# Two gather passes of a graph network on 16 of 17 edge tiles for 22 node blocks, each node's edge to itself taken from the products

## The reference, cut to what matters

```python
loop = jnp.arange(3125)
src = jnp.concatenate([s, d, loop]); dst = jnp.concatenate([d, s, loop])
o = jnp.argsort(dst, stable=True); src, dst = src[o], dst[o]

x = ln(x + gin(x))          # 4 times: h = x + segment_sum(x[src], dst); x = relu(h@W1+b1)@W2+b2
x = ln(x + rgcn(x))         # kinds of edge_type_8, each kind's mean, x@root
x = ln(x + attentive(x))    # srcs = alphas[rels] * (x @ w_rel)[rels, src], segment-summed; + x@update per edge
x = ln(x + gated(x))        # msg = (x@W + bias)[rel, src] * sigmoid(gate), segment-summed; + x@loop
```

## Time and profile before

| | |
|---|---|
| median of 3 runs | 2251.13 us (2251.12 to 2251.75) |
| the profiled execution, own time | 2252.56 us |
| its span | 2250.8 us |
| busy share of PE, PEld, DVE, ACT, POOL | 65%, 44%, 40%, 27%, 60% |
| chain that ended last | POOL 50%, PE 21%, issue 18%, ACT 5% |
| L1013 on POOL, passes 2 and 3 | 832 gathers, 954 ns each |
| L1315 on PE, the dense layers | 2100 matmuls, 406.8 us |

### The profile page before, as it was taken

One profiled execution on the slowest core, in us unless ns is written; L12 is line 12 of the kernel. 1 busy time (PEld: TensorE's weight loads), 2 busy tenths in 40 slices (PEclk: granted clock), 3 DMA queues, 4 the chain that ended last, 5 costly groups with the idle time before them and its releaser, 6 DMA issues.

```text
span 2250.8 us, 31616 instructions
## 1 busy us (share of the span) xinstructions
PE 1463.2 (65%) x7538; PEld 989.7 (44%) x7539; DVE 906.3 (40%) x2269; ACT 599.7 (27%) x1689; POOL 1360.4 (60%) x1574
## 2 busy tenths in 40 slices
PE   4776999999987777777764655555455433434433
PEld 2332554545456665666653533343333333323333
DVE  7887122213673444444445533333344212212212
ACT  3776000000023333333331644444343000000000
POOL 5000166720007777777777777777777777777775
PEclk8888999999988989989897876667677756565565
DMA  1000011100213333333333222222222222222221
GB/s 31 0 0 10 15 9 12 11 3 0 59 54 109 94 113 112 95 112 110 95 113 97 72 81 79 71 80 79 71 81 84 56 56 56 55 56 56 55 56 46
DMA packets 126652, 137.49 MB, mean 61 GB/s; under 512 B 80706, under 2 KB 97866, under 8 KB 123433
## 3 DMA queue, kind: packets, MB, share of 16 engines
q0 software_dynamic: 40896, 81.94, 13.9%
q1 hardware_dynamic: 85673, 54.54, 8.1%
HBM read 91.88 MB, written 44.52 MB: 61 GB/s over the span
## 4 chain that ended last, share of the span: by engine, by line
POOL 50%; PE 21%; issue 18%; ACT 5%; DVE 2%; ACTq 1%; DMA 1%; POOLq 1%; SPq 0%; DVEq 0%
POOL adj L1013 49%; PE acc L1315 18%; ACT adj L1714 5%; PE misc L1251 1%; PE acc L1586 1%; PE acc L1202 1%; ACTq L1707 1%; DVE adj L2607 0%; DMA adj<-table,adj 0%; DVE adj L2606 0%; ACTq L1714 0%; POOLq L1009 0%; PE acc L1251 0%; ACT adj L1773 0%; PE acc L1204 0%
## 5 line engine op out<-in xcount | busy, mean ns | idle before, releaser
L1013 POOL DMA_INDIRECT adj<-table,adj x832 | 793.5, 954 | 253.6 <-issue 252.9
L1586 PE MATMUL acc<-adj 128*128 x1760 | 364.5, 385 | 499.7 <-DMA adj<-table,adj 253.3
L1586 PEld LDWEIGHTS acc<-adj 128*128 128x128 f32 x1760 | 328.5, 285 | 560.3 <-issue 560.2
L1013 POOL DMA_INDIRECT adj<-tablex,adj x416 | 392.8, 944 | 210.9 <-issue 126.5
L1773 ACT ACTIVATE adj<-adj 128x128 f32<-128x128 f32 x832 | 264.5, 390 | 581.0 <-DMA adj<-tablex,adj 315.2
L1315 PE MATMUL acc<-adj,feat 128*128 (+1 forms) x2100 | 406.8, 354 | 8.4 <-issue 8.4
L1513 PE MATMUL acc<-adj 128*128 128x128 f32 x1664 | 245.3, 310 | 124.1 <-ACT adj L1773 113.9
L1997 DVE TENSOR_TENSOR adj<-acc,drel 128x768 f32<-128x768 f32 (+1 forms) x148 | 139.9, 948 | 423.6 <-PE acc L1586 423.3
L1513 PEld LDWEIGHTS acc<-adj 128*128 128x128 f32 x1664 | 228.8, 220 | 167.2 <-issue 167.1
L1315 PEld LDWEIGHTS acc<-adj,feat 128*128 (+1 forms) x2100 | 186.2, 98 | 217.1 <-issue 13.1
L959 POOL TENSOR_TENSOR node_rep<-node_rep,compb 128x128 f32<-128x128 f32 x128 | 58.5, 457 | 272.4 <-DMA node_rep<-in_L_gnn_weight_dram 263.5
(11 more groups left out here) (352 smaller groups left out, 1297.6 us busy)
## 6 DMA issues: line engine op xcount, KB each, us to landing
table<-adj SPq DMA_DIRECT2D x24, 1024.0 KB, 4.1
adj<-table,adj POOLq DMA_INDIRECT x834, 2.5
table<-adj SPq DMA_DIRECT2D x25, 512.0 KB, 2.9
adj<-tablex,adj POOLq DMA_INDIRECT x416, 2.5
table<-adj SPq DMA_DIRECT2D x25, 64.0 KB, 2.0
out_dram<-adj SPq DMA_DIRECT2D x24, 64.0 KB, 1.5
temp<-in_x_dram SPq DMA_DIRECT2D x4, 256.0 KB, 3.1
wrel<-node_rep SPq DMA_DIRECT2D x16, 64.0 KB
```

What stands on the lines that cost most here:

```text
L1013: pool.indirect_dma_start(ring[:, p_, 0:D], None, rows_, bass.IndirectOffsetOnAxis(ap=gidx[:, p_:p_ + 1], axis=0)).then_inc(msgs_in[third_ ...
L1586: last = nc.tensor.matmul(acc[:, bass.ds(blk[s], width)], hot[:, c, j, :], ring_flat[:, bass.ds(place[s], width)], start=False, stop=True, ...
```

## The change

In passes 2 and 3, tile 7 of the turns 2 to 23 (22 of 25; `LB = 2`, `LN = 22`) is no longer gathered, weighted or multiplied. Each of the 128 nodes of that turn's block has its loop edge somewhere in the tiles; the loop edges are taken out of the lists, and the edges of tile 7 are put in their places ("holes"). What a loop edge adds is taken from the products, which are on the chip anyway: `table_parts` picks each node's row of its own kind, 16 chained operations of 128 by 128 a block in pass 1 and 8 in pass 2, and `block_sum` of pass 2 adds the picked row by its weight.

To find the holes, the program now does this beside the dense layers:

- SP loads the list of destinations again, moved by one (`next1_i`, 3 DMAs, now in `ends_in`), waits for all nine, and writes the tiles' first nodes to DRAM; DVE puts five operations more on 104 by 512 into the check.
- DVE packs the edges' codes (`code_lists`); POOL then issues six DMAs, among them every eighth element of the list of destinations to DRAM (6640 pieces of 4 bytes) and two loads of 128 by 22 pieces of 4 bytes, before its first slice.
- Three searches follow, each 22 gathers on POOL (`found_rows`) and some counting on DVE: `loop_nodes`, `loop_eighths` and `loop_holes`. `loop_eighths` stands on DVE ahead of `merge(1)`, and `loop_holes` ahead of `merge(2)`.
- 66 scatters on POOL, three for each emptied tile, each after the last of its kind has landed, put codes and nodes in place. SP then loads them with four DMAs, where there was one.
- `EARLY_SLICES` becomes 9, 4, 3, and the 28 scatters of `edges_part` come after all slices. The load of the moved edges into the lists goes from layer 3 to turn 2 of pass 1, with `loops_taken`.

```diff
-EARLY_SLICES = (range(0, 6), range(6, 11), range(11, 16), ())
+EARLY_SLICES = (range(0, 9), range(9, 13), range(13, 16), ())
...
-                    for j in range(SIZES[c]):
+                    for j in range(SIZES[c] - (1 if c == 1 and emptied(ph, u) else 0)):
...
-                with pool.Fori(0, LAYERS // 2) as l:
-                    for q in range(SLICES // LAYERS):
-                        weights_slice(l, q)
-                pool.wait_ge(late_counted, PLACES_SET)
-                with pool.Fori(LAYERS // 2, LAYERS - 1) as l:
-                    for q in range(SLICES // LAYERS):
-                        weights_slice(l, q)
-                        edges_part(q)
...
+                pool.wait_ge(late_counted, LISTS_SET)
+                pool.dma_start(edge_codes[0:P * TILES, :].rearrange("(p t) o -> p (t o)", p=P)[:, FROM_TILE:TILES], tile16[:, FROM_TILE:TILES]
+                               ).then_inc(loops_in, 16)
+                pool.dma_start(edge_nodes[0:P * STEPS, :].rearrange("(p s) o -> p (s o)", p=P), step_nodes).then_inc(loops_in, 16)
+                pool.dma_start(eighths[0:TILES - 1, :].rearrange("t e -> (t e)"), bass.AP(dst.tensor, dst.offset, [[P // 16, (TILES - 1) * (P // 8)], [1, 1]])
+                               ).then_inc(loops_in, 16)
+                for k, o in ((0, here_i), (1, behind_i)):
+                    pool.dma_start(o, bass.AP(dst.tensor, dst.offset + emptied_tile(0) * P + k, [[1, P], [TPT * P, LN], [1, 1]])).then_inc(edges_in, 16)
+                pool.wait_ge(ends_in, ENDS_IN + 16)
+                pool.wait_ge(loops_in, 3 * 16)
+                pool.dma_start(firsts_b, first_list.partition_broadcast(P)).then_inc(edges_in, 16)
+                slices(0, 9)
+                pool.wait_ge(late_counted, NODES_SET)
+                found_rows(lambda b: sixteen[:, b, :], eighths, row_i)
+                slices(9, 13)
+                pool.wait_ge(late_counted, EIGHTS_SET)
+                found_rows(lambda b: eight[:, b, :], dst[0:E // 8 * 8].rearrange("(r e) -> r e", e=8), row_i)
+                slices(13, 16)
+                pool.wait_ge(late_counted, HOLES_SET)
+                found_rows(lambda b: found[:, b:b + 1], edge_codes, row_i)
+                for n in range(SWAPPED // 4):
+                    edges_part(n)
+                pool.wait_ge(loops_in, 3 * 16 + 3 * LN * 16)
+                for b in range(LN):
+                    if b > 0:
+                        pool.wait_ge(edges_in, (3 + b) * 16)
...
+                    pool.wait_ge(edges_out, (SWAPPED + b) * 16)
...
                 for l in range(LAYERS):
+                    if l == 0 and not general:
+                        code_lists()
                     if l == 1 and not general:
+                        loop_nodes()
                         edge_places()
+                        loop_eighths()
+                    if l == 2 and not general:
+                        loop_holes()
                     if l < LAYERS - 1:
                         merge(l)
...
+                        for r in range(R2):
+                            rows_ = stage[:, b.r, r * D:(r + 1) * D]
...
+                                ins = nc.vector.scalar_tensor_tensor(mine, rows_, of_r, mine, ALU.mult, ALU.add)
```

More of the change, by code:

```diff
@@ L409, in gnn @@
         zerob = sb("zerob", [P, KB], BF16)
+        hole = zerob[:, :].bitcast(F32)
+        here_i, behind_i, slot_c, slot_d, row_i, node_i, found = (hole[:, i * LN:(i + 1) * LN].bitcast(I32) for i in range(7))
+        here_f, node_f, tile_f, place_n, ends_f = (hole[:, i * LN:(i + 1) * LN] for i in (0, 7, 8, 9, 10))
+        more_f, many_f = (place_f[:, i * LN:(i + 1) * LN] for i in range(2))
+        loop_i = late[:, 2 * SWAPPED:2 * SWAPPED + LN].bitcast(I32)
+        assert 11 * LN <= KB // 2 and LN <= SWAPPED and 2 * LN <= 4 * 15
         epst = sb("epst", [P, 1])
@@ L655, in tiles_from, with emptied, picks, full_turns @@
             return u.num(TPT, PARTS_AT[c])
-        def msgs_before(ph, u, c):
-            uses = sum(uses_in(q, third_of(ph, u), c) for q in range(1, ph))
-            return u.third(16 * SIZES[c], 16 * SIZES[c] * uses)
+        def emptied(ph, u):
+            return ph > 1 and (not isinstance(u.k, int) or LB <= u.num() < LB + LN)
+        def picks(b):
+            return not isinstance(b.k, int) or LB - 1 <= b.num() < LB + LN
+        def full_turns(r):
+            return sum(1 for i in (*range(LB), *range(LB + LN, TURNS)) if i % AHEAD_T == r)
+        def tiles_in_pass(ph, r, c):
+            n = uses_in(ph, r, c)
+            if ph == 1 or c != 1:
+                return n * SIZES[c]
+            return n * (SIZES[c] - 1) + full_turns((r - ph + 1) % AHEAD_T)
+        def msgs_upto(ph, u, c):
+            before = sum(tiles_in_pass(q, third_of(ph, u), c) for q in range(1, ph))
+            if ph == 1 or c != 1:
+                return u.third(16 * SIZES[c], 16 * (before + SIZES[c]))
+            full = full_turns(u.r) - (1 if u.r == (TURNS - 1) % AHEAD_T and not u.last() else 0)
+            return u.third(16 * (SIZES[c] - 1), 16 * (before + SIZES[c] - 1 + full))
         def uses_in(ph, r, c):
@@ L1769, in take @@
                     return
-                hold(act, msgs_in[third_of(ph, u)][c], msgs_before(ph, u, c) + 16 * SIZES[c])
-                for j in range(SIZES[c]):
+                hold(act, msgs_in[third_of(ph, u)][c], msgs_upto(ph, u, c))
+                for j in range(SIZES[c] - (1 if c == 1 and emptied(ph, u) else 0)):
                     o = ring[:, place_of(ph, u, c) + j, 0:D]
@@ L2274, in edge_places, with code_lists @@
                 nc.vector.engine_nop().then_inc(late_counted, 1)
+            def code_lists():
+                codes, kind = tile16[:, FROM_TILE:TILES], split[:, 0:TILES - FROM_TILE].bitcast(I32)
+                place(nc.vector.tensor_copy(kind, tile8[:, FROM_TILE:TILES]))
+                place(nc.vector.tensor_single_scalar(kind, kind, R1 - 1, ALU.bitwise_and))
+                nc.vector.tensor_copy(step_nodes, drel[:, :])
+                place(nc.vector.scalar_tensor_tensor(codes, codes, float(R1), kind, ALU.mult, ALU.add))
+                nc.vector.engine_nop().then_inc(late_counted, 1)
@@ L2477, in table_parts @@
                     last.then_inc(rows_set, 1)
+                    if not general:
+                        hold(dve, rows_set, b.num(1, 1))
+                        hold(dve, prod_free[SIDE], blocks_seen(2, b, 1))
+                        for r in range(R3):
+                            if r > 0:
+                                dve.wait_ge(picked, b.num(R3, PICKS2 + r + min(max(b.num(1, 1 - LB), 0), LN)) if isinstance(b.k, int)
+                                            else b.num(R3 + 1, PICKS2 + r + 1 - LB))
+                            nc.vector.scalar_tensor_tensor(own, stage[:, b.r, r * D:(r + 1) * D],
+                                                           own_kind3[:, bass.ds(b.num(), 1), r:r + 1].rearrange("p b r -> p (b r)"), own,
+                                                           ALU.mult, ALU.add).then_inc(picked, 1)
             def one_pass(ph, general):
```

237 lines of the change are left out of this document (198 added, 39 removed).

## The result

The changed kernel took 2485.4 us in the median of 4 runs (2480.8 to 2486.0); the kernel before took 2251.4 beside it (2251.1 to 2253.3). The ratio is 1.103, with a 95% interval of 1.101 to 1.105. The forecast was slower, 2333, between 2305 and 2405: the direction held, the size did not. 234 us were added, not 80.

A forecast was written before the change was run, and what follows sets the result against it. POOL's gathers were taken to bound the passes, PE the stretch before. To 2252.6 us it added 5.0 (start), 93.1 + 25 (POOL's queue and X), 3 (clock), 9.6 (DVE tails), less 55.4 (gathers): 2333, range 2305 to 2405.

The forecast's parts named there:

- Where it is decided: On POOL before pass 1: clearing `near_i` stands behind the new work, comes 93.3 us + X late, and delays pass 1.
- three signs: Forecast wrong if clearing comes before 640, PE doesn't wait in layer 1, or passes 2 and 3 turns take 17 gathers' time.
- The gain: Passes 2 and 3, on POOL: 44 gathers fewer at 1.26 us each, 55.4 us less.
- the tail of 6.4: End of pass 2: DVE's added operations for blocks 22 and 23 and `block_sum` delay the table by 6.4 us, without slack.
- 66 scatters 83.2: POOL's queue before the clearing: 66 scatters take 83.2 us, priced from 28 earlier scatters at 977 ns plus some 0.3 between.
- The rival that said so: Scatters wait for their landing: at 5.0 us against 3.8 covered, 27 us more, 2360 in all; chance 0.10.
- With 42% busy and 51 tiles of ring ahead this costs nothing within the pass: Pass 1 on DVE: 16 picks, 5.6 us a turn, cost nothing within the pass, only where passes meet.
- The rival had 1 us a turn: DVE becomes late in pass 1 and PE with it: 1 us more in 22 turns, ring's lead used up, 2355; chance 0.05.
- X: Cost of POOL's six plain DMAs and their landing before the first slice: taken as 25 us, between 10 and 97.
- Layer 1: PE idles some 50 us at layer 1's join, as `merge(1)` stands behind `loop_eighths`; a later stall swallows it.
- Clearing to pass 1: From clearing to pass 1's first gather: 99.4 us, 96.5 before; 3.5 more for SP, 3.7 less for DVE's wait, 3 clock.
- the 3 for the clock: After PE's long stall in layer 3, 3 us added because matmuls after a long wait run slower at first.

The follow-up runs named there:

- e_eighths_late: The changed kernel with `loop_eighths` moved behind `merge(1)` on DVE instead of ahead of it; 2496.9 us, 11.5 us more than the changed kernel.
- e_all17: The changed kernel with its search, scatters and picks kept, but passes 2 and 3 gather, weight and sum all 17 tiles again; 2527.1 us.
- e_spaced: The changed kernel with every wait kept, but `loop_codes` laid out with 64 bytes from word to word instead of 4; 2374.8 us.
- e_all_fixed: The changed kernel with unwaited scatters, spaced `loop_codes`, clearing ahead of scatters, reordered POOL and SP, and pass 1's picks in two halves; 2236.8 us.
- e_bykind: The changed kernel's 66 scatters issued kind after kind, each waiting for the one right ahead of it; 2574.3 us.
- e_reorder: The changed kernel with slices moved ahead of POOL's waits, SP's loads to match, and `loop_eighths` behind `merge(1)`; 2464.8 us.

## Why the prediction was right and wrong

- *Where it is decided*, the clearing of `near_i` behind POOL's new work: right. e_clear_first moves the clearing ahead of the scatters, with SP's loads of what they wrote, and the start of pass 1 comes 83 us earlier; e_eighths_late shows that a stall of PE ahead of it does not count. So "slower" was right for the forecast's own reason and not by luck. None of the three signs that I had named for a wrong forecast came: all three look for a smaller cost than forecast or for a missing gain, and the clearing was later.
- *The gain*, 44 x 1.26 = 55.4 less the tail of 6.4: right. The piece became 51.9 us shorter, and e_all17 gives 54.4 back, which leaves 2.5 for the tail.
- *"66 scatters 83.2"*: the step that failed, 101.2 us of the miss. The price per issue was right (84.4 us in e_spaced, 1.28 each), but the sum left out the wait of each scatter for the last of its kind, as if the three issues since then, 3.8 us, covered the landing. The rival that said so had the mechanism and 5.0 us for the landing; it was 8.4, and 22 x (8.4 - 3.8) = 101 where I had 27. I took the one landing in the trace, 2.5 us of a gather, as if only the direction were new, and never asked which addresses the 128 words of a scatter had. The Trainium skill, DMA: Bandwidth & Descriptors, section "Anatomy of one DMA — SWDGE (gpsimd) path", puts most of a fixed time of about 2 us down to the receipt of the write. The 2.1 and 2.2 us of spread words agree with that; the 7.9 of words side by side are beyond it.
- *"With 42% busy and 51 tiles of ring ahead this costs nothing within the pass"*: the second step that failed, 42.3 us of the miss. A busy share, 42% or 63%, says nothing of a chain in which PE waits for DVE several times a turn: before the change DVE waited 88.6 us in 23 turns where the picks now stand, 3.9 a turn, and 5.6 us of picks do not fit into that. The ring only hid it until the pass ended. (For the two last blocks the sum has a slip: 2 x 5.6 - 2.8 - 2.7 is 5.7, not 5.5.) The rival had 1 us a turn; 45.5 / 22 is 2.1. Two rivals came true together, and neither sum had room for that.
- *X*, 25: 32.4 measured. Of it 7.0 are issues, and `eighths` with its 6640 pieces took only 2.29 us of POOL. The same section of the skill calls the generation of descriptors "small, variable", and the trace agrees. POOL's wait for the landing ended 28 us behind the issue of `eighths`, where 31 ns a piece gave 13. The 5632 pieces of `here_i` and `behind_i` followed it in the same queue, and I had not counted them; with them the same rate gives 24, an estimate that no run tests. The range, up to X = 45 in the forecast's own, held it.
- *Layer 1*: "some 50 us" was 51.3, for half of the reason. 32.1 of it was not `loop_eighths` but SP, whose load of the weights of the next layer stood behind the stores of nine slices. I had followed POOL's queue and not SP's.
- *Clearing to pass 1*: 6 more. DVE begins on `near_i` at 817.55, 15.6 us behind the clearing, where it was 5.2. SP had to see the last scatter land and issued its first load 5.4 us behind the clearing, and of the four loads ahead one took 2.23 us, not 0.4. From DVE's start to the first gather it is 89.8 us, 91.4 before: there the 3 for the clock and the 3.7 that a wait of DVE was to give back come out within 1 us.

## What to carry to other kernels

The landing of a scatter can hang on where its words go: 128 words took 2.2 us or 7.9 here. Before a scatter's completion is waited for, look at how its addresses lie. Work added to an engine inside a chain is priced by the wait in which it stands, not by the engine's busy share: the same picks cost 3.5 us in two halves, and 45.5 or 91.6 in one piece. And work that is "beside" something holds up whatever stands behind it in its queue, and SP's queue of loads is one too: it kept PE for 32.1 us in layer 1 and for 31.7 in e_all_fixed.

## What the runs showed of the hardware

- An indirect scatter of 128 words of 4 bytes to DRAM landed 7.9 us after its issue with the words next to each other (e_bykind), and 2.2 with 64 bytes from word to word (e_spaced). That the cause is writes to the same small piece of memory is my reading; the runs show the layout and the time. The Trainium skill, DMA: Bandwidth & Descriptors, section "Specifications", says that transfers below 512 bytes are done by reading, modifying and writing; size alone does not make the difference here, since both have 4 bytes.
- In the order of the changed kernel that landing differed from run to run, 7.8 to 8.5 us in the median, and the 66 scatters took 171.5 to 187.8. Where scatters are waited for, pieces are to be compared, not whole times.
- 12,272 pieces of 4 bytes cost POOL 5.05 us of issue in three DMAs, and POOL's wait for the first of them, 6640 pieces from DRAM to DRAM, ended 28 us after its issue. A load that SP began to issue meanwhile took SP 18.74 us of issue instead of 0.9 and kept POOL waiting for 21 (e_reorder).
